# Runs of 64 small products on TensorE, early row mixing on VectorE, and a loop of 28 steps in an RWKV layer with experts

## The chip, the cores and the metric

One Trainium2 chip, one core of it. The metric is the device time of one execution in microseconds (us). The kernel before has a median of 6792.22 us over three runs (6789.73 to 6812.12).

## The reference, what matters of it

The layer has two parts. The first is a time-mixing layer over x of 2 x 4096 rows of 512 channels: rows are mixed with the row before them (`xx = xprev - x`, `xxx = x + xx * time_maa_x`, a small network that gives four deltas, and four mixed inputs `x + xx * (time_maa + delta)`), projected to r, k, v, a gate and several low-rank terms, and run through a recurrence for each of 16 heads of 32 channels:

```
sab = S @ kk
S = S * exp(w) + sab b^T + v k^T
y = S @ r
```

The output is normalised by head, gets a bonus term and the gate, and is projected. The second part is a layer norm with a balanced assignment of 1024 rows to each of 8 experts (512 to 2048 to 512, gelu). The change is in the first part alone.

## The kernel before

The first part goes over 64 tiles. A tile is 64 rows of each of the two sequences, 128 rows together, and lies in memory as 128 channels by 4 groups of 128 columns. The recurrence is solved in chunks of 32 rows: for each of 16 units (group, sequence, chunk) and 4 heads there is a triangular 32x32 system, whose inverse is built by doubling in four levels. A level `lev` is, for each of the 64 systems, a product P (`ub` by `inv`) on TensorE (`P_of`, L842), a copy of it out of PSUM on ScalarE (`part_of`, L605), a product Q (that copy by `invT`) on TensorE (`Q_of`, L858), and on VectorE a masked copy into `invT` (step C.T) and a transposition to `inv` (step C.I) (`invert`, L400). Each product is a 32x32 tile of the array, so that four heads run side by side.

The work is a pipeline over turns. In one turn five stages run, each on another tile: N (row statistics), A (mixing and projections), B (keys, queries and scores for the inverse and the outputs), C (the inverse and the recurrence) and D (norm, gate, output). `step` (L1121) writes one turn for all engines. The order on each engine is written out by hand: in `on_vector` (L340), `on_scalar` (L601), `on_gpsimd` (L762) and `on_tensor` (L821), each of which executes in order, and in the lists `DVE_STEPS`, `ACT_STEPS`, `POOL_STEPS` and `PE_STEPS` that number the steps. A wait on a step is a wait on a semaphore of its engine. PSUM banks are shared in the order of the table `BANK`; `clear` (L333) waits until the last reader of a bank's previous tenant is done.

Five turns are written out, then a loop with a body of four turns runs 14 times, then seven turns are written out (L1138 to L1147). `SETS = 4` sets of semaphores rotate, so the body is a multiple of four.

TensorE's order in a turn, with the names used below: transposition of x (L956, step A.x); a quarter of the values (L829); the first half of P0 (L853, 32 products); a quarter of the values; centre (L969); the second half of P0; mix (L977), which needs VectorE's xxx (L444); the scores for the experts (L983); Q0 (L864) in halves around values; var (L995), delta (L932), gate; P1 in halves around values; bonus (L1016); gate1 and low_wa (both L838), which need the mixed inputs xf0 and xf1 (L398); delta3; Q1 in halves around the score block u0 (L877); u1, u2; P2 in halves around low_k (L838, needs xf2); key (L829); Q2 in halves around u3; key; P3 in halves around decay (L1055); u4, u5; Q3 in halves around low2 (L1071); y0, y1; then the recurrence over two chunks (L891, L905, L915, L924) with y2 to y5, the output projection (L947) and receptance between.

VectorE's order at the start of a turn: query and key spans B.dq, B.dk3, B.dk2 (L349, L354); N's statistics (L436, L438); xx and xxx (L441, L444); B.dk1, B.dk0; keys kb3, kk3 (L360, L363); rated (L457); invert(0); mixed input 0 (L392, L398); D.normed; keys 2; mixed input 1; keys 1 and 0; bonus (L477); C.uk (L413); D.bonus (L483), D.gated (L487); the mask of u0 (L377); invert(1); mixed input 2; mask of u1; mixed input 3, and so on.

Of the kernel before, what the change touches and what calls it, by code (L numbers as in the profile page):

```python
# [8 lines left out]
P = 128  # L9
# [9 lines left out]
SETS = 4  # L19

# [95 lines left out]
def time_mix(nc, core, dram):  # L116
# [3 lines left out]
    with ExitStack() as ctx:  # L120
# [119 lines left out]
        for g in range(G):  # L240
# [16 lines left out]
            "A.carried A.x B.ek3 B.ek012 C.P0 A.mix D.squares B.eq D.lnv N.lnv D.rstd N.rstd B.v C.P1 A.hid_g A.hid_w A.hid_a "  # L257
# [5 lines left out]
            "A.x D.centre C.P0 A.mix A.scored C.Q0 D.var A.delta D.gate B.value C.P1 B.bonus A.gate1 A.low_wa A.delta3 B.u0 C.Q1 "  # L263
            "B.u1 B.u2 A.low_k C.P2 B.u3 C.Q2 A.key A.decay C.P3 B.u4 B.u5 A.low2 C.Q3 B.y0 B.y1 A.sums C.z0 B.y2 "
            "B.y3 C.u0 C.y0 D.out B.y4 B.y5 C.z1 C.u1 A.recept C.y1").split()
# [74 lines left out]
        def on_vector(e, turn, on, out, got):  # L340
# [88 lines left out]
            enter(e, dve, "dve", turn)  # L429
            if Bs:  # L430
                query_span()
                key_span(3)
                key_span(2)
# [5 lines left out]
            if A:  # L439
                e.wait_ge(act.sem, act["A.x"])  # L440
                e.tensor_tensor(by_b(xx), xs[:, :, :, 0:TB], xnow, ALU.subtract).then_inc(dve.sem, dve.step("A.xx"))  # L441
                e.wait_ge(dve.sem, dve["A.xx"])
                for g in range(G):
                    e.scalar_tensor_tensor(  # L444
                        grp(xxx, g).rearrange("p (b t) -> p b t", b=B), grp(xx, g).rearrange("p (b t) -> p b t", b=B),
                        wt["maa_x"][:, g:g + 1], xs[:, g, :, 1:TB + 1], ALU.mult, ALU.add).then_inc(
                        dve.sem, dve.step(f"A.xxx{g}"))
# [20 lines left out]
            if Bs:  # L468
                make_keys(2)
            if A:  # L470
                lerp_of(1)
            if Bs:
                make_keys(1)
                make_keys(0)
                e.wait_ge(act.sem, act["B.v"])
                e.wait_ge(pe.sem, pe["B.bonus"])
                e.tensor_tensor(col(bonuses[(turn - 1) % SETS]), col(BANK["bonus"]), col(v), ALU.mult).then_inc(  # L477
                    dve.sem, dve.step("B.bonus"))
            if Cs:
                turn_scores([(1, "uk")])  # L480
# [7 lines left out]
            if Bs:  # L488
                mask_scores("u", 0)
            if Cs:  # L490
                invert(1)
            if A:
                lerp_of(2)
            if Bs:
                mask_scores("u", 1)
# [105 lines left out]
        def on_scalar(e, turn, on, out, got):  # L601
# [26 lines left out]
            if Bs:  # L628
                e.wait_ge(dve.sem, dve["B.dk3"])
                e.activation(key_units(1, 3), key_units(1, 3), ACT.Exp).then_inc(act.sem, act.step("B.ek3"))  # L630
                e.wait_ge(dve.sem, dve["B.dk0"])
                e.activation(by_key[:, :, 1, 0:key_at(3)], by_key[:, :, 1, 0:key_at(3)], ACT.Exp).then_inc(
                    act.sem, act.step("B.ek012"))
            if Cs:
                part_of(0)
            if A:
                e.wait_ge(pe.sem, pe["A.mix"])
                e.activation(col(mix), BANK["mix"][:, 0:P], ACT.Tanh).then_inc(act.sem, act.step("A.mix"))
            if D:
# [181 lines left out]
        def on_tensor(e, turn, on, out, got):  # L821
# [20 lines left out]
            def P_of(lev, half):  # L842
                if half == 0:
                    clear(e, f"P{lev}")
                    if lev == 0:
                        if "C.rows1" in dve.was:
                            e.wait_ge(dve.old, dve.ago("C.rows1"))
                        e.wait_ge(dve.old, dve.ago("B.inv"))
                    else:
                        e.wait_ge(dve.sem, dve[f"C.I{lev - 1}"])  # L850
# [4 lines left out]
                if half:  # L855
                    mm.then_inc(pe.sem, pe.step(f"C.P{lev}"))

            def Q_of(lev, half):  # L858
                if half == 0:
                    clear(e, f"Q{lev}")  # L860
                    e.wait_ge(act.sem, act[f"C.P{lev}"])
                for n in range(half * U // 2, (half + 1) * U // 2):
# [3 lines left out]
                if half:  # L866
                    mm.then_inc(pe.sem, pe.step(f"C.Q{lev}"))
# [103 lines left out]
            if Cs:  # L971
                P_of(0, 1)
# [13 lines left out]
            if Cs:  # L986
                Q_of(0, 0)
            if Bs:
                value_of(2, 3)
            if Cs:  # L990
                Q_of(0, 1)
# [14 lines left out]
            if Cs:  # L1006
                P_of(1, 0)
            if Bs:
                value_of(3, 4).then_inc(pe.sem, pe.step("B.value"))
            if Cs:  # L1010
                P_of(1, 1)
# [11 lines left out]
            if Cs:  # L1023
                Q_of(1, 0)
            if Bs:
                score("u", 0)
            if Cs:
                Q_of(1, 1)
            if Bs:
                score("u", 1)  # L1030
                score("u", 2)
            if Cs:
                P_of(2, 0)
            if A:
                low("low_k", 2)
            if Cs:
                P_of(2, 1)
            if A:
                clear(e, "key")
                key_of(0, 2)  # L1040
            if Cs:
                Q_of(2, 0)
            if Bs:
                score("u", 3)
            if Cs:
                Q_of(2, 1)
            if A:
                key_of(2, 4).then_inc(pe.sem, pe.step("A.key"))
            if Cs:
                P_of(3, 0)  # L1050
# [7 lines left out]
            if Cs:  # L1058
                P_of(3, 1)
# [3 lines left out]
            if Cs:  # L1063
                Q_of(3, 0)
# [9 lines left out]
            if Cs:  # L1074
                Q_of(3, 1)
# [25 lines left out]
            if Bs:  # L1101
                score("y", 4)
                score("y", 5)
# [606 lines left out]
```

## Time and profile before

| what | value |
|---|---|
| median of three runs | 6792.22 us |
| the profiled execution's own time | 6799.37 us |
| its span, first to last instruction | 6797.6 us |
| granted TensorE clock, mean over the span | 0.949 |
| first part, TensorE transposes x of tile 0 at | 31.7 us |
| the same of the last tile at | about 4661 us |
| busy over the span: PE, PEld, DVE, ACT, POOL | 89%, 64%, 59%, 28%, 21% |

How to read it: PE is TensorE's matmuls, PEld its weight loads, DVE is VectorE, ACT is ScalarE, POOL is GpSimd, SP is SyncE. A turn of the pipeline is counted from one transposition of x (L956) to the next. The matmul of an fp32 product shows as two records and two weight loads, so 32 products are "x64". "idle before" in brackets is the time in which the engine had nothing to run, and after the arrow stands what ended it; "issue" there means that nothing in the profile was waited for, PEq and DVEq are the sequencers, and L329 is the wait at the entry of a turn.

### The profile page before, as it was taken

The numbers are of one execution on the slowest core, as the hardware profiler recorded it, in microseconds if no ns is written. First come the engines' busy times: TensorE is split into PE (matmuls) and PEld (weight loads), VectorE is DVE, ScalarE is ACT, GpSimd is POOL, SyncE is SP. The second block draws the span as 40 slices with busy tenths as digits, with TensorE's granted clock in tenths as the row PEclk, the third lists the DMA queues.
The fourth block names the chain that finished last, engine by engine and source line by source line (L and its number), as shares of the span: only waits on it lengthen the run. The fifth ranks groups of instructions, "written<-read, shape, count | busy, mean of one in ns | idle before, by whom it ended". The sixth has DMA issues, their size and how long they took to land. (4 is left out here: it accounts for less than half of the span.)

```text
span 6797.6 us, 270041 instructions
## 1 busy us (share of the span) xinstructions
PE 6026.9 (89%) x123464; PEld 4343.0 (64%) x123464; DVE 4002.5 (59%) x9325; ACT 1878.1 (28%) x3531; POOL 1458.2 (21%) x1284
## 2 busy tenths in 40 slices
PE   6888888888889888888888888888489999999999
PEld 5777777777777777777777777777334444444444
DVE  5777777777777777777777777777442223222310
ACT  3333333333333333333333333333100000000000
POOL 1222122222212222221222222222021122112220
PEclk8999999999999999999999999999689999999999
DMA  1000000000000000000000000000212211221120
GB/s 54 16 20 16 16 22 16 16 18 20 16 16 22 16 16 18 20 16 17 21 16 16 18 20 16 17 21 11 69 44 70 77 55 62 71 67 65 56 76 13
DMA packets 108728, 212.84 MB, mean 31 GB/s; under 512 B 25424, under 2 KB 26704, under 8 KB 107088
## 3 DMA queue, kind: packets, MB, share of 16 engines
q1 hardware_dynamic: 92240, 144.98, 7.4%
q0 software_dynamic: 15360, 50.48, 2.2%
q8 instruction: 995, 16.30, 1.0%
q14 instruction: 133, 1.09, 0.1%
HBM read 144.67 MB, written 50.72 MB: 29 GB/s over the span
## 5 line engine op out<-in xcount | busy, mean ns | idle before, releaser
L377 DVE COPY_PREDICATED time_raw<-time_known,w_bank 128x96 f32<-128x96 int32 (+6 forms) x3072 | 826.0, 273 | 226.5 <-PE w_bank L877 146.8
L1662 PE MATMUL moe_bank<-moe_w,moe_hidden 128*128 128x512 f32 x2048 | 928.7, 596 | 0.0
L1649 PE MATMUL moe_bank<-moe_hT,moe_w 128*128 128x512 f32 x2048 | 923.2, 594 | 0.8 <-DVE moe_hT L1549 0.8
L1649 PEld LDWEIGHTS moe_bank<-moe_hT,moe_w 128*128 128x128 f32 x2048 | 386.3, 190 | 471.2 <-issue 470.1
L1662 PEld LDWEIGHTS moe_bank<-moe_w,moe_hidden 128*128 128x128 f32 x2048 | 379.4, 190 | 429.5 <-issue 428.1
L1570 ACT ACTIVATE moe_hidden<-moe_bank,moe_b 128x512 f32<-128x512 f32 x256 | 175.9, 687 | 1628.2 <-PE moe_bank L1649 1523.1
L806 POOL TENSOR_TENSOR time_tail<-time_tail,time_lp 128x512 f32<-128x512 f32 x64 | 75.4, 1178 | 2414.1 <-ACT time_lp L733 2350.3
L864 PE MATMUL w_bank<-time_invT,time_part 32*32 32x32 f32 x32768 | 437.1, 204 | 71.5 <-issue 50.2
L402 DVE COPY_PREDICATED time_invT<-time_levels,w_bank 128x512 f32<-128x512 int32 x256 | 187.1, 731 | 499.7 <-PE w_bank L864 499.7
L864 PEld LDWEIGHTS w_bank<-time_invT,time_part 32*32 32x32 f32 x32768 | 373.0, 116 | 152.9 <-issue 98.3
L853 PE MATMUL w_bank<-time_inv,time_ub 32*32 32x32 f32 x32768 | 401.5, 196 | 77.6 <-ACT time_yT L617 30.6
L853 PEld LDWEIGHTS w_bank<-time_inv,time_ub 32*32 32x32 f32 x32768 | 342.3, 107 | 195.2 <-issue 117.1
L774 POOL TENSOR_TENSOR time_queries_u<-time_dq,time_kkn 32x512 f32<-32x512 f32 x256 | 304.4, 1189 | 553.1 <-ACT time_dq L648 538.0
L877 PE MATMUL w_bank<-time_keys,time_queries_u 128*128 128x160 f32 x2048 | 385.1, 329 | 34.8 <-DVE time_mixed L487 14.5
L877 PE MATMUL w_bank<-time_keys,time_queries_y 128*128 128x160 f32 x2048 | 338.7, 313 | 59.0 <-DVE time_mixed L552 53.0
L877 PEld LDWEIGHTS w_bank<-time_keys,time_queries_y 128*128 128x128 f32 x2048 | 290.3, 193 | 121.6 <-DVE time_mixed L552 104.3
L1549 DVE COPY moe_hT<-moe_bank 128x512 f32<-128x512 f32 x64 | 44.2, 691 | 535.6 <-PE moe_bank L1636 535.6
L829 PE MATMUL w_bank<-time_xf,time_value 128*128 128x128 f32 x2048 | 355.8, 328 | 0.1
L774 POOL TENSOR_TENSOR time_queries_y<-time_dq,time_r 32x512 f32<-32x512 f32 x256 | 349.4, 1365 | 26.2 <-POOL time_queries_u L774 10.8
L877 PEld LDWEIGHTS w_bank<-time_keys,time_queries_u 128*128 128x128 f32 x2048 | 306.5, 201 | 63.4 <-DVE time_mixed L487 20.1
L392 DVE SCALAR_TENSOR_TENSOR time_lerp<-w_bank,time_maa,time_xx 128x128 f32<-128x128 f32 x1024 | 284.5, 339 | 64.5 <-PE w_bank L932 64.4
L829 PEld LDWEIGHTS w_bank<-time_xf,time_value 128*128 128x128 f32 x2048 | 307.8, 230 | 9.6 <-PE w_bank L924 0.2
(227 smaller groups left out, 10038.5 us busy)
## 6 DMA issues: line engine op xcount, KB each, us to landing
moe_w<-in_w SPq DMA_DIRECT2D x64, 1024.0 KB, 7.3
mid_xn<-time_xn_rows SPq DMA_DIRECT2D x128, 129.0 KB, 2.5
time_x_rows<-in_x SPq DMA_DIRECT2D x128, 128.0 KB, 2.8
time_base<-in_x SPq DMA_DIRECT2D x128, 128.0 KB, 3.3
mid_acc<-time_mixed SPq DMA_DIRECT2D x128, 128.0 KB, 2.7
mid_scores<-time_rated SPq DMA_DIRECT2D x128, 2.0 KB, 2.2
moe_b<-in_b SPq DMA_DIRECT2D x8, 256.0 KB
time_receptance<-in_w_receptance SPq DMA_DIRECT2D x1, 1024.0 KB, 4.8
```

Source lines behind the costliest of these rows:

```text
L377: e.copy_predicated(by_raw[:, "uy".index(q), n0:n1, :, 0:8 * j + 8], known[:, "uy".index(q), :, :, mine].to_broadcast([P, n1 - n0, 2, 8 * ...
L392: e.scalar_tensor_tensor(grp(lerp, g), grp(BANK[f"delta{f}"], g), wt["maa"][:, f * G + g:f * G + g + 1], grp(xx, g), ALU.add, ALU.mult).th ...
L402: e.copy_predicated(chunks(got["invT"]), level(lev + 1, U), chunks(BANK[f"Q{lev}"])).then_inc(dve.sem, dve.step(f"C.T{lev}"))
L774: e.tensor_tensor(heads_of(q)[head(h), :, h], by_block(dq)[head(h), :, :, at:at + 8], eights(by)[head(h)], ALU.mult).then_inc(pool.sem, po ...
L806: e.tensor_tensor(chunks(tail), chunks(tail), padded(lp)[:, :, 1:33], ALU.add).then_inc(pool.sem, pool.step("A.lt"))
L829: mm = e.matmul(ps[:, o * P:(o + 1) * P], weight[:, g * width + o * P:g * width + (o + 1) * P], rhs_of(g), start=g == 0 and (o == 0 or not ...
L853: mm = e.matmul(BANK[f"P{lev}"][head(h), blk(n)], got["ub"][head(h), blk(n)], got["inv"][head(h), blk(n)], start=True, stop=True, skip_gro ...
L864: mm = e.matmul(BANK[f"Q{lev}"][head(h), blk(n)], part[head(h), blk(n)], got["invT"][head(h), blk(n)], start=True, stop=True, skip_group_c ...
L877: mm = e.matmul(BANK[f"{q}{m}"][:, (n - n0) * 2 * KEYS:(n - n0 + 1) * 2 * KEYS], queries[q][:, n * P:(n + 1) * P], keys[:, n * 2 * KEYS:(n ...
L1570: e.activation(hidden[now % 4][:, :], up[now % 3][:, :], ACT.Gelu_apprx_tanh, bias=b1[:, x * FC + k:x * FC + k + 1]).then_inc(act.sem, act ...
L1649: got = e.matmul(up[now % 3][:, :], w1[:, g * F + k * P:g * F + (k + 1) * P], hT[x % 2][:, g * CAP + half * HALF:g * CAP + (half + 1) * HA ...
L1662: got = e.matmul(down[t][:, :], hidden[now % 4][:, t * P:(t + 1) * P], tile(w2, k), start=k == 0, stop=k == FC - 1)
```

## The change

1. `P_of` and `Q_of` lose their halves: the 64 products of a level stand in one run. What lay between two halves now lies before or after.
2. TensorE's order is rewritten: both first quarters of the values come before P0, centre after it; value(3,4) after P1; u0 and u1 after Q1, then P2, low_k, the first half of key, u2, Q2, the second half of key, u3, P3, decay, u4, u5, Q3, low2. y5 comes before y4.
3. VectorE computes xx and xxx first in a turn, ahead of the spans and the statistics. Mixed input 1 comes ahead of keys 2. invert(1) and mixed input 2 come ahead of C.uk and of the masks of u0 and u1.
4. ScalarE does the copy of P0 and the tanh of mix ahead of the exponential B.ek012, which waits for B.dk0.
5. The loop has a body of 28 turns, executed twice, instead of four turns 14 times.

```diff
+LONG = 28
@@ VectorE
             enter(e, dve, "dve", turn)
+            if A:
+                ...
             if Bs:
                 query_span()
                 key_span(3)
...
+            if A:
+                lerp_of(1)
             if Bs:
                 make_keys(2)
-            if A:
-                lerp_of(1)
-            if Bs:
                 make_keys(1)
                 make_keys(0)
...
-            if Cs:
-                turn_scores([(1, "uk")])
             if D:
                 ...
+            if Cs:
+                invert(1)
+            if A:
+                lerp_of(2)
+            if Cs:
+                turn_scores([(1, "uk")])
             if Bs:
                 mask_scores("u", 0)
-            if Cs:
-                invert(1)
-            if A:
-                lerp_of(2)
-            if Bs:
                 mask_scores("u", 1)
@@ ScalarE
                 e.activation(key_units(1, 3), key_units(1, 3), ACT.Exp).then_inc(act.sem, act.step("B.ek3"))
+            if Cs:
+                part_of(0)
+            if A:
+                ...
             if Bs:
                 e.wait_ge(dve.sem, dve["B.dk0"])
                 ...
-            if Cs:
-                part_of(0)
-            if A:
-                ...
@@ TensorE
-            def P_of(lev, half):
...
-                for n in range(half * U // 2, (half + 1) * U // 2):
+            def P_of(lev):
...
+                for n in range(U):
                     for h in range(HG):
                         mm = e.matmul(BANK[f"P{lev}"][head(h), blk(n)], got["ub"][head(h), blk(n)], got["inv"][head(h), blk(n)],
...
-                value_of(0, 1)
-            if Cs:
-                P_of(0, 0)
-            if Bs:
-                value_of(1, 2)
+                value_of(0, 2)
+            if Cs:
+                P_of(0)
...
             if Bs:
+                score("y", 5)
                 score("y", 4)
-                score("y", 5)
@@ loop
-        with nc.Fori(0, tiles // SETS - 2) as four:
-            for i in range(SETS):
-                step(four * SETS + (i + 1), SETS + 1 + i, "NABCD")
+        turns = (tiles - 8) // LONG
+        with nc.Fori(0, turns) as part_of_tiles:
+            for i in range(LONG):
+                step(part_of_tiles * LONG + (i + 1), SETS + 1 + i, "NABCD")
```

## Rows read from the trace of the kernel before

**Rows 1.** Windows: stretch, us; busy PE, PEld, DVE, ACT, POOL; clock; DMA.
```profile
200.00:4661.00 4461.00, 3904.05 (x110999) 3257.69 (x110996) 3228.78 (x7800) 1581.32 (x3060) 1027.89 (x900) 0.95 0.07 18
```
**Rows 2.** Waits of PE in 200:4661: who for whom, us in total, times, longest.
```profile
PE w_bank L977 <- DVE time_lerp L444: 133.6, 53, 2.8
PE w_bank L838 <- DVE time_xf L398: 79.5, 60, 2.1
PE w_bank L838 <- DVE time_raw L377: 58.6, 60, 1.0
PE w_bank L877 <- DVE time_mixed L552: 51.3, 60, 0.9
PE w_bank L956 <- PEq L329: 46.3, 13, 3.8
PE w_bank L864 <- issue: 43.9, 47, 1.7
PE w_bank L853 <- issue: 19.4, 24, 1.2
```
**Rows 3.** Windows of two turns: the first after a jump back, the other not.
```profile
2064.00:2134.50 70.50, 64.67 (x1850) 53.91 (x1850) 51.70 (x127) 25.72 (x49) 15.98 (x14) 0.95 0.08 19
2208.40:2283.80 75.40, 64.81 (x1850) 54.15 (x1850) 53.32 (x131) 26.49 (x51) 16.95 (x15) 0.95 0.07 17
```
**Rows 4.** Timeline, PE, a turn without jump: start, length, what, [idle before].
```profile
1689.53 0.66 PE L956 MATMUL w_bank<-time_ident,time_xn_rows 128*128 128x128 f32 x4
...
1697.62 1.41 PE L977 MATMUL w_bank<-time_lerp,time_maa_w 128*128 128x128 f32 x8 [2.79 <-DVE time_lerp L444]
...
1701.37 2.08 PE L829 MATMUL w_bank<-time_xf,time_value 128*128 128x128 f32 x8
```
**Rows 5.** Timeline, PE, start of a turn after a jump back.
```profile
2064.30 1.08 PE L956 MATMUL w_bank<-time_ident,time_xn_rows 128*128 128x128 f32 x4 [3.36 <-PEq L329]
...
2074.59 1.16 PE L829 MATMUL w_bank<-time_xf,time_value 128*128 128x128 f32 x8
```
**Rows 6.** Timeline, PE, halves of a level and what lies between them.
```profile
1728.52 0.75 PE L864 MATMUL w_bank<-time_invT,time_part 32*32 32x32 f32 x64
1729.21 2.05 PE L829 MATMUL w_bank<-time_xf,time_key_w 128*128 128x128 f32 x16
1731.19 0.75 PE L853 MATMUL w_bank<-time_inv,time_ub 32*32 32x32 f32 x64
...
1733.64 1.35 PE L877 MATMUL w_bank<-time_keys,time_queries_u 128*128 128x160 f32 x8
1735.48 0.82 PE L864 MATMUL w_bank<-time_invT,time_part 32*32 32x32 f32 x64 [0.48 <-ACT time_part L607]
...
1737.37 0.55 PE L864 MATMUL w_bank<-time_invT,time_part 32*32 32x32 f32 x41
1739.33 0.39 PE L864 MATMUL w_bank<-time_invT,time_part 32*32 32x32 f32 x23 [1.41 <-issue]
```
**Rows 7.** Timeline, DVE, the start of the turn of rows 4.
```profile
1692.32 0.72 DVE L427 TENSOR_TENSOR time_state<-time_grown,time_faded 128x256 f32<-128x256 f32 x1
...
1696.33 1.14 DVE L444 SCALAR_TENSOR_TENSOR time_lerp<-time_xx,time_maa_x,time_x 128x128 f32<-128x128 f32 x4
...
1698.64 0.69 DVE L363 TENSOR_TENSOR time_keys<-time_keys,time_k 128x512 f32<-128x512 f32 x1
...
1710.39 1.44 DVE L363 TENSOR_TENSOR time_keys<-time_keys,time_k 128x384 f32<-128x384 f32 x1
...
1714.83 0.68 DVE L477 TENSOR_TENSOR time_bonus<-w_bank,time_v 128x512 f32<-128x512 f32 x1
```
**Rows 8.** Timeline, ACT, the copy of P0 in that turn.
```profile
1698.79 0.57 ACT L607 COPY time_part<-w_bank 128x512 f32<-128x512 f32 x1
```
**Rows 9.** The page: busy time and records; a DMA queue's packets, MB, share.
```profile
PE 6026.9 (89%) x123464; PEld 4343.0 (64%) x123464; DVE 4002.5 (59%) x9325; ACT 1878.1 (28%) x3531; POOL 1458.2 (21%) x1284
...
q8 instruction: 995, 16.30, 1.0%
```

More of the change, by code:

```diff
@@ L256, in time_mix @@
         ACT_STEPS = (
-            "A.carried A.x B.ek3 B.ek012 C.P0 A.mix D.squares B.eq D.lnv N.lnv D.rstd N.rstd B.v C.P1 A.hid_g A.hid_w A.hid_a "
+            "A.carried A.x B.ek3 C.P0 A.mix B.ek012 D.squares B.eq D.lnv N.lnv D.rstd N.rstd B.v C.P1 A.hid_g A.hid_w A.hid_a "
             "D.affine0 D.affine1 D.affine2 D.affine3 A.hid_kkk A.hid_mk C.P2 A.exp_z A.tail A.k C.P3 A.tna A.tnma "
@@ L262, in time_mix @@
         PE_STEPS = (
-            "A.x D.centre C.P0 A.mix A.scored C.Q0 D.var A.delta D.gate B.value C.P1 B.bonus A.gate1 A.low_wa A.delta3 B.u0 C.Q1 "
-            "B.u1 B.u2 A.low_k C.P2 B.u3 C.Q2 A.key A.decay C.P3 B.u4 B.u5 A.low2 C.Q3 B.y0 B.y1 A.sums C.z0 B.y2 "
-            "B.y3 C.u0 C.y0 D.out B.y4 B.y5 C.z1 C.u1 A.recept C.y1").split()
+            "A.x C.P0 D.centre A.mix A.scored C.Q0 D.var A.delta D.gate C.P1 B.value B.bonus A.gate1 A.low_wa A.delta3 C.Q1 B.u0 "
+            "B.u1 C.P2 A.low_k B.u2 C.Q2 A.key B.u3 C.P3 A.decay B.u4 B.u5 C.Q3 A.low2 B.y0 B.y1 A.sums C.z0 B.y2 "
+            "B.y3 C.u0 C.y0 D.out B.y5 B.y4 C.z1 C.u1 A.recept C.y1").split()
         BANK = Banks(psum, [
@@ L429, in on_vector @@
             enter(e, dve, "dve", turn)
+            if A:
+                e.wait_ge(act.sem, act["A.x"])
+                e.tensor_tensor(by_b(xx), xs[:, :, :, 0:TB], xnow, ALU.subtract).then_inc(dve.sem, dve.step("A.xx"))
+                e.wait_ge(dve.sem, dve["A.xx"])
+                for g in range(G):
+                    e.scalar_tensor_tensor(
+                        grp(xxx, g).rearrange("p (b t) -> p b t", b=B), grp(xx, g).rearrange("p (b t) -> p b t", b=B),
+                        wt["maa_x"][:, g:g + 1], xs[:, g, :, 1:TB + 1], ALU.mult, ALU.add).then_inc(
+                        dve.sem, dve.step(f"A.xxx{g}"))
             if Bs:
@@ L438, in on_vector @@
                 e.bn_aggr(mv[:, :], stats[:, :]).then_inc(dve.sem, dve.step("N.mv"))
-            if A:
[L440 to L447, printed above, removed]
             if Bs:
@@ L467, in on_vector @@
                 e.tensor_tensor(col(mixed), col(BANK["centre"]), col(rstd), ALU.mult).then_inc(dve.sem, dve.step("D.normed"))
-            if Bs:
-                make_keys(2)
             if A:
@@ L472, in on_vector @@
             if Bs:
+                make_keys(2)
                 make_keys(1)
@@ L487, in on_vector @@
                 e.tensor_tensor(col(mixed), col(mixed), col(BANK["gate"]), ALU.mult).then_inc(dve.sem, dve.step("D.gated"))
-            if Bs:
-                mask_scores("u", 0)
             if Cs:
@@ L493, in on_vector @@
                 lerp_of(2)
+            if Cs:
+                turn_scores([(1, "uk")])
             if Bs:
+                mask_scores("u", 0)
                 mask_scores("u", 1)
@@ L630, in on_scalar @@
                 e.activation(key_units(1, 3), key_units(1, 3), ACT.Exp).then_inc(act.sem, act.step("B.ek3"))
-                e.wait_ge(dve.sem, dve["B.dk0"])
-                e.activation(by_key[:, :, 1, 0:key_at(3)], by_key[:, :, 1, 0:key_at(3)], ACT.Exp).then_inc(
-                    act.sem, act.step("B.ek012"))
             if Cs:
@@ L638, in on_scalar @@
                 e.activation(col(mix), BANK["mix"][:, 0:P], ACT.Tanh).then_inc(act.sem, act.step("A.mix"))
+            if Bs:
+                e.wait_ge(dve.sem, dve["B.dk0"])
+                e.activation(by_key[:, :, 1, 0:key_at(3)], by_key[:, :, 1, 0:key_at(3)], ACT.Exp).then_inc(
+                    act.sem, act.step("B.ek012"))
             if D:
@@ L840, in low @@
                 mm.then_inc(pe.sem, pe.step("A." + name))
-            def P_of(lev, half):
[L843 to L850, printed above, removed]
-                for n in range(half * U // 2, (half + 1) * U // 2):
+            def P_of(lev):
+                clear(e, f"P{lev}")
+                if lev == 0:
+                    if "C.rows1" in dve.was:
+                        e.wait_ge(dve.old, dve.ago("C.rows1"))
+                    e.wait_ge(dve.old, dve.ago("B.inv"))
+                else:
+                    e.wait_ge(dve.sem, dve[f"C.I{lev - 1}"])
+                for n in range(U):
                     for h in range(HG):
@@ L854, in P_of, with Q_of @@
                                       start=True, stop=True, skip_group_check=True)
[L855 to L862, printed above, removed]
+                mm.then_inc(pe.sem, pe.step(f"C.P{lev}"))
+            def Q_of(lev):
+                clear(e, f"Q{lev}")
+                e.wait_ge(act.sem, act[f"C.P{lev}"])
+                for n in range(U):
                     for h in range(HG):
@@ L865, in Q_of @@
                                       start=True, stop=True, skip_group_check=True)
-                if half:
-                    mm.then_inc(pe.sem, pe.step(f"C.Q{lev}"))
+                mm.then_inc(pe.sem, pe.step(f"C.Q{lev}"))
             def score(q, *which):
@@ L970, in on_tensor @@
                     pe.sem, pe.step("D.centre"))
-            if Cs:
-                P_of(0, 1)
             if A:
@@ L986, in on_tensor @@
             if Cs:
-                Q_of(0, 0)
+                Q_of(0)
             if Bs:
                 value_of(2, 3)
-            if Cs:
-                Q_of(0, 1)
             if D:
@@ L1006, in on_tensor @@
             if Cs:
-                P_of(1, 0)
+                P_of(1)
             if Bs:
                 value_of(3, 4).then_inc(pe.sem, pe.step("B.value"))
-            if Cs:
-                P_of(1, 1)
             if Bs:
@@ L1023, in on_tensor @@
             if Cs:
-                Q_of(1, 0)
+                Q_of(1)
             if Bs:
                 score("u", 0)
+                score("u", 1)
             if Cs:
[L1028 to L1033, printed above, removed]
+                P_of(2)
             if A:
                 low("low_k", 2)
-            if Cs:
-                P_of(2, 1)
             if A:
@@ L1040, in on_tensor @@
                 key_of(0, 2)
+            if Bs:
+                score("u", 2)
             if Cs:
-                Q_of(2, 0)
+                Q_of(2)
+            if A:
+                key_of(2, 4).then_inc(pe.sem, pe.step("A.key"))
             if Bs:
@@ L1045, in on_tensor @@
             if Cs:
-                Q_of(2, 1)
-            if A:
-                key_of(2, 4).then_inc(pe.sem, pe.step("A.key"))
-            if Cs:
-                P_of(3, 0)
+                P_of(3)
             if A:
@@ L1057, in on_tensor @@
                 mm.then_inc(pe.sem, pe.step("A.decay"))
-            if Cs:
-                P_of(3, 1)
             if Bs:
@@ L1063, in on_tensor @@
             if Cs:
-                Q_of(3, 0)
+                Q_of(3)
             if A:
@@ L1073, in on_tensor @@
                 mm.then_inc(pe.sem, pe.step("A.low2"))
-            if Cs:
-                Q_of(3, 1)
             if Bs:
```

8 rows, old and new, of the table DVE_STEPS are left out of this document.

## The prediction

> **What bounds the kernel now.** I read first how the time divides: one window over the 60 full turns of the first part. It holds 4461 us, 74.4 us a turn, and TensorE is busy for 3904 of them, VectorE for 3229 (53.8 a turn), ScalarE and GpSimd for far less [rows 1]. The rest of the span, the experts and the ends, is untouched but for the few turns at both ends, which I leave out. So the question is a turn of TensorE, times 60. It is not all work: each turn has some 9 us without a matmul, and the clock is 0.95 on average, which is a tenth of the time at 1.2 GHz instead of 2.4, some 3.7 us of work lost in a turn of 74.4.
>
> Second, the waits of PE, divided by 60 [rows 2]. The largest is that of mix (L977) for xxx, 133.6 us, 2.2 a turn, and nearly 2.8 in each turn without a jump. Then low_wa for xf1, 79.5 (1.3); low_k for xf2, listed under the mask that ran just after it, 58.6 (1.0); y4 for the addition into acc, 51.3 (0.85); the jump back, 46.3 (13 times 3.6). The rows named "issue" wait for no other engine: 43.9 and 19.4, 1.06 a turn.
>
> Third, two turns side by side [rows 3]: the one after a jump takes 70.5 us, the other 75.4, with the same busy PE to 0.2 us. The turn after the jump is short because VectorE has caught up: mix has no wait of 2.79. The jump's cost is thus largely given back in this kernel, and taking it away alone would bring little. It is worth its price only because xxx is also made earlier.
>
> Fourth, the clock. In the turn without a jump TensorE idles before mix, and then the 8 records of the values at L829 take 2.08 us [rows 4]; after a jump the same 8 take 1.16 [rows 5]. The slow stretch at the start follows that idle time.
>
> **The change part by part**, in us of a turn, against 74.4.
>
> *xx and xxx first.* VectorE ends the last turn's state at 1693.04, 3.5 after TensorE's L956 at 1689.53; from xx to mix it is two steps, 0.69 (taken from a step of equal size, L363) and 1.14, with the hand-over some 2.0 [rows 4, 7]. Mix can start at 5.5 instead of 8.1. Ahead of it TensorE has the transposition (0.5), 16 records of values (1.98), P0 (1.2, below) and centre (about 1.0): 4.7. A wait of about 1.0 stays, with ends 0.5 and 1.5. Against 2.2 and a wait of the first half of P0 of about 0.5 for the last copy of the turn before, now covered by the second quarter of the values: **-1.7**.
>
> *The jump.* 12 of 13 go: 46.3 x 12/13 / 60 = **-0.7**. The rest of each body was streamed before as it is now: 16.3 MB over the queue of instructions, about 66 bytes for each of TensorE's 247 thousand matmul and load records [rows 9], more than a body of four could keep.
>
> *The clock.* If the idle stretch before mix shrinks to 1.0, the slow stretch behind it should mostly go; other gaps of 1.0 to 1.4 us stay, and new ones come. Ends: nothing, and all 3.7. I take **-2.0**.
>
> *Runs of 64.* The second half of a run costs what its records cost inside one: x64 takes 0.75 and x41 takes 0.55, 8.7 ns each, so 0.56 for 64, against a start-to-start of 0.69 for a half [rows 6]. The neighbours join too: 16 records take 2.05 and 8 take 1.16, so one visit less saves 0.2 (2 x 1.16 less 2.05, less the overlap of 0.07 of lengths) [rows 5, 6]. Together 0.13 + 0.2 = 0.33, eight times: **-2.6**. Ends: 0.1 and 0.4 each, -0.8 and -3.2.
>
> *Mixed input 1 ahead of keys 2.* These keys are 0.9 and 1.44 long [rows 7], so xf1 comes 2.3 earlier and low_wa's 1.3 go: **-1.3**. Low_k: xf2 is ready some 1.8 after C.I1 ends, and P2 covers 1.2 of it instead of 0.7: **-0.4**. y5 ahead of y4 puts 0.65 under the wait of 0.85 for acc, but then the copy of y out of PSUM is barely late: **-0.4**.
>
> New waits. *Q0* needs the copy of P0, on ScalarE behind the exponential of dk3, which VectorE now makes after xxx: 5.35 for xxx, two spans 1.25, exponential 0.65, copy 0.57 [rows 8], hand-overs: 8.0. TensorE is at 7.4. **+0.6**, ends 0 and 1.4. *u0* needs the bonus and all keys. From the end of delta TensorE has gate, P1, values, bonus, gate1, low_wa, delta3 and Q1: six visits of about 1.05 and two runs, 8.7. VectorE has xf0, normed, xf1, six key steps and the bonus: 8.7 to 10. The spread is what POOL does to it: the key step of 384 columns took 1.44 beside the queries of GpSimd, the one of 512 took 0.69 without [rows 7]. **+1.0**, ends 0.2 and 1.6. *Q3*: ScalarE comes to the copy of P3 after three operations on decay and key. Now Q3 waits 0.48 with half of P3 and u4, u5 ahead of it [rows 6]; the half is gone from there: **+0.8**, ends 0 and 1.3. The masks of u0 come later than C.T1 and xf2 but before u2 needs their bank: nothing. SyncE waits for rated and acc as before, and neither moves by more than 1 us: nothing.
>
> *Instructions.* The stalls named issue fall in the dense places: 23 records of Q3 came 1.41 late, in the middle of a run [rows 6]. A product is four PE records here; at 66 bytes a record a packet of 16 KB is about 250 of them, which is one run of 64 products. 995 packets take 1.0% of 16 engines, 1.1 us each [rows 9]. A turn needs 3700 records, 15 packets, one per 4.6 us at a turn of 69; a run now eats one in 1.2 us, a half ate half of one in 0.7. Stalls now cost 1.06; I take them to double and a little: **+1.2**. The ends are -1.06 (all gone) and 8 x 1.41 less 1.06, +10.2, if each run stops once; I stay near today's rows as the mean demand grows by only 8%.
>
> The Trainium skill speaks to this place: Runtime: NRT & Kernel Launch, section Instruction fetch mechanics, says that instructions come in blocks of 16 KiB, that crossing into the next is mostly hidden, and that a taken branch out of the window costs a fetch. The 3.36 of idle time at the jump agrees. The 1.41 inside straight code does not, and by the page alone the +1.2 would be 0 or less; that is the second rival below.
>
> Sum: -1.7 - 0.7 - 2.0 - 2.6 - 1.3 - 0.4 - 0.4 = -9.1; +0.6 + 1.0 + 0.8 + 1.2 = +3.6; net -5.5, a turn of 68.9. Sixty turns: -330. The profiled execution took 6799.4, so 6469; it lies 7 above the median, so **6462**.
>
> **The rivals.**
> First, **instructions bound the runs** (slower). Each run of 64 products stops once for its packet, as Q3 did, 1.41 each: 11.3 a turn instead of 2.3. The net is then +3.5 to the turn, +210: about 7000. It decides from 6.7 a turn of added stall, 0.8 for each run. For it: the stalls stand in dense places already. Against: only 71 issue waits of 0.9 on average over 60 turns in these two rows, with 16 half runs a turn. 4%.
> Second, **instructions are hidden**: the stalls go away with the idle places before the runs as slack: 2.3 less a turn, 66.6: 6325. For it: the other waits let the sequencer run ahead; against: the 1.41. 12%.
> Third, **VectorE becomes what is late**: 53.8 busy in 69 is 78%, and its order is a chain with TensorE's. If the bonus comes 1.6 late and its delay carries into u1, P2, low_k with another 1.5, the turn is 71.0: 6590. For it: the slowed key steps; against: its idle time at Q0 and Q2 is several us. 16%.
> Fourth, **the clock does not recover**: gaps of 1.0 before mix, 0.6 before Q0, then four around u0 to low_k, keep as much of the turn at 1.2 GHz: +2.0, 6582. 13%.
>
> **How the numbers follow.** The forecast has 55%, the rivals 4, 12, 16 and 13. The unknown costs around the forecast (clock 1.7 either way, runs 1.0, u0 and Q3 1.0, instructions 1.0) come to about 2.3 a turn together, 140 us. 6340 to 6620 holds the third and fourth rival and most of the forecast's spread. About 0.3% is what a measurement of this kernel can tell from no change; only the first rival is slower by that, and no change would need the terms to cancel: 95% faster, 1% same, 4% slower.
>
> **What would show it.** Right: mix's wait near 1.0 and none of 2.8; low_wa without a wait; turns all alike with no jump but one; clock of a turn at 0.97 or more; rows of 128 records for P and Q in about 1.3; issue waits of about 2 a turn. Wrong: Q and P rows broken in two by issue waits of over 1 in most turns (first rival); a wait of u0 for the bonus beyond 1.6 and of low_k beyond 1 (third); a clock of 0.95 (fourth).

## The result: 6739.6 us against 6792.2, and 6462 was forecast

The changed kernel takes 6739.57 us (median of five runs, 6734.03 to 6745.69), a ratio of 0.9918 to the kernel before, 95% interval 0.9901 to 0.9934. It is faster, as forecast, but by 53 us, 0.8%, and not by 330, and it lies outside the stated range of 6340 to 6620. The profiled execution took 6739.65 us, its span is 6737.7 us, the mean clock 0.937 against 0.949.

First the window over the same 60 turns as [rows 1], in the kernel after.

```profile
197.50:4596.80 4399.30, 3840.92 (x111001) 3249.24 (x111001) 3298.81 (x7801) 1571.59 (x3060) 1024.52 (x900) 0.93 0.07 18
```

A turn is 73.3 us against 74.4; forecast were 68.9. The busy time of PE fell by 63 us, 1.05 a turn; the time in which it idles is 557 us before and 558 after, 9.3 a turn. The clock is 0.93, not higher than 0.95. So nothing of the idle time was won. Of the work more was won than the busy time shows: busy time times clock, as an estimate, is 61.8 us a turn before and 59.5 after, but the lower clock took about half of that back. The waits of PE show where the idle time went; columns as in [rows 2], stretch 200:4600, nearly the window above.

```profile
PE w_bank L852 <- issue: 132.6, 82, 2.8
PE w_bank L861 <- issue: 113.3, 77, 2.8
PE w_bank L861 <- DVE time_raw L378: 59.9, 53, 1.4
PE w_bank L873 <- DVE time_bonus L477: 44.3, 34, 2.1
PE w_bank L969 <- DVE time_lerp L436: 40.7, 38, 1.3
PE w_bank L1051 <- issue: 28.7, 16, 2.7
PE w_bank L861 <- ACT time_part L606: 21.0, 45, 0.7
PE w_bank L873 <- DVE time_mixed L551: 19.3, 60, 0.7
...
PE w_bank L829 <- issue: 17.6, 19, 2.5
PE w_bank L838 <- DVE time_xf L399: 14.4, 39, 0.5
...
PE w_bank L952 <- PEq L330: 3.5, 1, 3.5
```

Against [rows 2]: mix (now L969) waits 40.7 us instead of 133.6, low_wa and low_k (L838) 14.4 instead of 138.1, y4 (after L551) 19.3 instead of 51.3, the jump 3.5 instead of 46.3. All the rows that name another engine or the jump come to 237 us, 4.0 a turn; they were 447, 7.5 a turn. And all the rows "issue" come to 313 us, 5.2 a turn, where before they were 98, 1.6 a turn. (Q3's wait for ScalarE's copy of P3 stands in the row of time_raw L378: a mask happened to end last before it.) What the other engines gave back went into stalls in which TensorE waits for none of them.

The timeline of PE shows where they stand; in brackets the idle time before.

```profile
1253.78 1.50 PE L829 MATMUL w_bank<-time_xf,time_key_w 128*128 128x128 f32 x12
1255.12 0.98 PE L873 MATMUL w_bank<-time_keys,time_queries_u 128*128 128x160 f32 x6
1256.04 1.29 PE L852 MATMUL w_bank<-time_inv,time_ub 32*32 32x32 f32 x128
1257.25 0.38 PE L1037 MATMUL w_bank<-time_hid_w,time_decay_w 96*128 96x128 f32 x1
1259.15 1.47 PE L1037 MATMUL w_bank<-time_hid_w,time_decay_w 96*128 96x128 f32 x7 [1.53 <-issue]
1260.42 2.34 PE L873 MATMUL w_bank<-time_keys,time_queries_u 128*128 128x160 f32 x8
1263.08 1.13 PE L861 MATMUL w_bank<-time_invT,time_part 32*32 32x32 f32 x111 [0.32 <-DVE time_raw L378]
1266.46 0.44 PE L861 MATMUL w_bank<-time_invT,time_part 32*32 32x32 f32 x17 [2.26 <-issue]
1266.83 2.09 PE L1051 MATMUL w_bank<-time_hid,time_low_w 32*128 32x128 f32 x32
```

P3 (L852) runs through in 1.29 us, the price that the prediction put on a run: 128 records in one piece, against two pieces of 0.75 with their visits. One record of decay later TensorE stands for 1.53 us. It does 7 records of decay, 8 of u4 and u5 and 111 of Q3 and stands again, 2.26 us, in the middle of a run. From stall to stall that is 126 matmul records; a window over it counts 127 weight loads as well:

```profile
1259.15:1266.46 7.31, 4.73 (x126) 4.26 (x127) 2.66 (x9) 2.25 (x4) 0.00 (x0) 0.77 0.01 2
1314.30:1322.72 8.42, 4.80 (x126) 4.02 (x127) 8.11 (x19) 0.00 (x0) 0.73 (x2) 0.80 0.01 2
```

The second row is the same between two other stalls, in the middle of Q1 and in the middle of P2, with the same counts. 253 records and a few semaphore instructions are one packet of the instruction queue: the page gives it 977 packets with 16.01 MB, so 16.4 KB each, and 64 to 66 bytes a record. The stalls stand where one packet ends. Counted with the semaphore instructions, all 159 issue stalls of more than 0.8 us in the 60 turns lie whole multiples of 256 instructions apart, with one shift, at the jump. A packet ends in a place, not after a time: in the second row TensorE ran out of instructions 7.0 us after the packet's first record, with two waits for VectorE in between, and the next packet was late by 1.42 us all the same.

The DMA view shows when the late packets move. The first line is 1259.15:1264.10, the next two 1264.10:1264.20:

```profile
DMA packets 0, 0.00 MB, mean 0 GB/s; under 512 B 0, under 2 KB 0, under 8 KB 0
DMA packets 1, 0.02 MB, mean 164 GB/s; under 512 B 0, under 2 KB 0, under 8 KB 0
q8 instruction: 1, 0.02, 59.1%
```

So the packet starts at 1264.1, when TensorE has all but finished the one before it; TensorE stands from 1264.20 and goes on at 1266.46. In the second case nothing moves in 1314.30:1320.40 and one packet starts in 1320.40:1320.50; TensorE stands from 1321.3 and goes on at 1322.72. Other transfers can't have held these two up, as there were none. In all 159 stalls TensorE goes on 2.2 to 2.9 us after such a packet starts, and 1.2 to 1.7 us after it ends.

Behind these two stalls the clock falls. A window before them, one behind each, and what lies between (last columns: clock, DMA share, GB/s):

```profile
1251.00:1257.00 6.00, 6.00 (x273) 5.62 (x273) 5.21 (x15) 0.00 (x0) 0.00 (x0) 1.00 0.02 5
1259.70:1263.10 3.40, 3.08 (x17) 2.71 (x16) 1.24 (x6) 2.25 (x4) 0.00 (x0) 0.51 0.00 0
1263.10:1266.40 3.30, 1.10 (x111) 1.01 (x112) 1.43 (x4) 0.00 (x0) 0.00 (x0) 1.00 0.02 5
1266.50:1269.90 3.40, 3.40 (x53) 3.11 (x53) 2.04 (x3) 0.91 (x2) 0.00 (x0) 0.51 0.02 5
1270.00:1276.00 6.00, 6.00 (x149) 4.83 (x148) 3.18 (x11) 2.50 (x7) 0.00 (x0) 1.00 0.16 46
1322.72:1326.12 3.40, 3.40 (x51) 3.35 (x51) 2.92 (x10) 1.21 (x3) 0.00 (x0) 1.00 0.02 5
```

In the stretches behind the two the clock is 0.51, the lower of its two levels, 1.2 and 2.4 GHz. Not every stall does this: the last row is the stretch behind the stall of 1.42 us, at 1.00. The 8 records of u4 and u5 took 2.34 us in such a stretch; before they took 1.35 [rows 6].

### The profile page after: what moved, and what is told of

Read it like the earlier page. It is cut to its first block and busy times, and to the rows that moved or that the text cites. A ratio compares the mean times of both kernels' runs of the same rounds, so it can differ in the third digit from the quotient of the medians.

```text
span 6737.7 us, 269852 instructions
## 1 busy us (share of the span) xinstructions
PE 5964.4 (89%) x123464; PEld 4335.2 (64%) x123464; DVE 4075.9 (60%) x9325; ACT 1868.0 (28%) x3531; POOL 1454.5 (22%) x1284
## 3 DMA queue, kind: packets, MB, share of 16 engines
q8 instruction: 977, 16.01, 1.0%
## 5 line engine op out<-in xcount | busy, mean ns | idle before, releaser
L378 DVE COPY_PREDICATED time_raw<-time_known,w_bank 128x96 f32<-128x96 int32 (+6 forms) x3072 | 828.4, 275 | 429.6 <-PE w_bank L873 343.6
L861 PE MATMUL w_bank<-time_invT,time_part 32*32 32x32 f32 x32768 | 362.8, 197 | 211.7 <-issue 122.1
L852 PE MATMUL w_bank<-time_inv,time_ub 32*32 32x32 f32 x32768 | 364.8, 197 | 155.1 <-issue 134.8
L861 PEld LDWEIGHTS w_bank<-time_invT,time_part 32*32 32x32 f32 x32768 | 326.2, 107 | 259.6 <-issue 163.2
L852 PEld LDWEIGHTS w_bank<-time_inv,time_ub 32*32 32x32 f32 x32768 | 326.8, 108 | 209.0 <-issue 193.5
L774 POOL TENSOR_TENSOR time_queries_u<-time_dq,time_kkn 32x512 f32<-32x512 f32 x256 | 312.0, 1219 | 484.5 <-ACT time_dq L648 469.5
L873 PE MATMUL w_bank<-time_keys,time_queries_y 128*128 128x160 f32 x2048 | 382.2, 335 | 28.3 <-DVE time_mixed L551 19.9
L873 PEld LDWEIGHTS w_bank<-time_keys,time_queries_u 128*128 128x128 f32 x2048 | 330.2, 214 | 96.5 <-DVE time_bonus L477 56.9
L873 PEld LDWEIGHTS w_bank<-time_keys,time_queries_y 128*128 128x128 f32 x2048 | 329.3, 211 | 91.6 <-issue 39.0
L829 PE MATMUL w_bank<-time_xf,time_value 128*128 128x128 f32 x2048 | 303.3, 300 | 12.2 <-issue 12.1
L829 PE MATMUL w_bank<-time_xf,time_key_w 128*128 128x128 f32 x2048 | 288.3, 299 | 6.8 <-issue 6.8
```

The source lines that it names most:

```text
L378: e.copy_predicated(by_raw[:, "uy".index(q), n0:n1, :, 0:8 * j + 8], known[:, "uy".index(q), :, :, mine].to_broadcast([P, n1 - n0, 2, 8 * ...
L774: e.tensor_tensor(heads_of(q)[head(h), :, h], by_block(dq)[head(h), :, :, at:at + 8], eights(by)[head(h)], ALU.mult).then_inc(pool.sem, po ...
L829: mm = e.matmul(ps[:, o * P:(o + 1) * P], weight[:, g * width + o * P:g * width + (o + 1) * P], rhs_of(g), start=g == 0 and (o == 0 or not ...
L873: mm = e.matmul(BANK[f"{q}{m}"][:, (n - n0) * 2 * KEYS:(n - n0 + 1) * 2 * KEYS], queries[q][:, n * P:(n + 1) * P], keys[:, n * 2 * KEYS:(n ...
```

## Experiments

Eleven kernels ran. Each has a ratio to the kernel before on the same chip. The theory: runs of 64 products take their instructions faster than packets come, and the stalls pull the clock down. The rivals: the new order of steps costs it, VectorE or ScalarE is late anyway, or the jumps were not worth removing.

**1. TensorE's order of before, the rest of the change.**

```diff
-                value_of(0, 2)
-            if Cs:
-                P_of(0)
+                value_of(0, 1)
+            if Cs:
+                P_of(0, 0)
+            if Bs:
+                value_of(1, 2)
...
```

> The changed kernel, but TensorE's order and the halves of P and Q as before (so VectorE's and ScalarE's new order and the loop of 28 stay). Theory: runs of 64 products (256 records) eat a packet of instructions faster than the next one comes, 5.3 us of issue waits a turn, and the idle places lower the clock. With halves the issue waits go back to about 1.6 a turn, the clock to 0.95 or more, mix and low_wa keep their short waits: a turn of 69 to 71, 6530 to 6620 us. Rival (runs of 64 are worth their 2.6 us a turn and the moved steps cost it): 2.6 us a turn slower than the change, about 6890.

Measured: 6908.58 us, ratio 1.0171 [1.0144, 1.0199]. The theory's number failed and the rival's was met, but for a reason that neither had. The waits of PE (200:4600):

```profile
PE w_bank L877 <- DVE time_raw L378: 205.1, 58, 4.2
PE w_bank L877 <- DVE time_bonus L477: 140.4, 57, 3.2
PE w_bank L864 <- issue: 65.3, 54, 1.7
```

The issue waits did fall, to some 1.8 us a turn. But in TensorE's old order u0 comes half a run earlier and u2 before P2, while VectorE now masks u0 after mixed input 2. So u0 waits 2.5 us a turn for the bonus, and u2 3.5 for the mask. The two orders belong together; this kernel undid too much at once. It shows that VectorE's later masks don't go with TensorE's old order; it says nothing of runs against halves.

**2 and 3. The loop.** A body of 4 in the changed kernel, and a body of 28 in the kernel before.

```diff
-LONG = 28
+LONG = 4
```

> The changed kernel with a loop body of 4 turns, executed 14 times. Theory: each jump back costs 3.5 us, 12 more of them 42; with xx first the turn after a jump wins little back (1 us each): 6765 to 6785. Rival (as in the kernel before, the turn after a jump gives all of it back): 6740.

> The kernel before with the loop of 28 turns and nothing else. Theory: the 12 jumps (3.5 us each, 42) go, but the 12 turns after them lose their head start (70.5 against 74.5): 6785 to 6805, no change. Rival: the jumps' time is gained, 6750.

Measured: 6755.19 us (6733.47 to 6768.89), 0.9936 [0.9914, 0.9959], against 0.9918 [0.9901, 0.9934] of the change; and 6787.65, 0.9992 [0.9982, 1.0003]. In the kernel before the loop is worth nothing, as its head start after a jump is paid back. In the changed kernel it is worth 16 us between medians, with intervals that overlap: between what the two expectations said, and not settled beyond "less than the 42 of the jumps". Its jumps take 44.5 us (PEq, 13 times), and part of that comes back: over its 60 turns mix waits 27.3 us in all instead of 40.7, and the issue rows come to 304 instead of 313.

**4 and 5. Few records.** Each run of 64 products becomes ten, and then five, products of 128x128x128. The inverse is left out in these two; all other steps stay.

```diff
-                for n in range(U):
-                    for h in range(HG):
-                        mm = e.matmul(BANK[f"P{lev}"][head(h), blk(n)], got["ub"][head(h), blk(n)], got["inv"][head(h), blk(n)],
+                for n in range(10):
+                    mm = e.matmul(BANK[f"P{lev}"][:, n % G * P:(n % G + 1) * P], grp(got["ub"], n % G), grp(got["inv"], n % G),
```

> The changed kernel with each run of 64 products of 32x32 (256 records of TensorE) replaced by 10 products of 128x128x128 (40 records), about as long (1.1 us); it leaves the inverse out, its levels are computed from other products. A turn has 1700 fewer records, all else is the same. Theory (instructions bound the runs, and their stalls pull the clock down): issue waits below 1 us a turn, clock 0.97 or more, a turn of 67 to 69.5, 6380 to 6520 us. Rival (the other engines are what is late, and TensorE would wait for them anyway): issue waits turn into waits for VectorE and ScalarE, a turn of 72 to 73, 6690 to 6740.

> As the run with ten products, but five of 128x128x128 (10 matmul records of 0.11 us, 1.1 us) in the place of each run of 64; ten were 2.2 us and so 1 us a run too long, 8 us a turn. The inverse is left out. Theory: no issue waits, clock 0.98 or more, and the 8 us fall away but for what VectorE and ScalarE are then late: a turn of 64 to 68, 6170 to 6420 us. Rival (the full clock of the run with ten products came from its longer work, not from the missing stalls): clock 0.95 or less and a turn of 68 to 70, 6420 to 6550.

Measured: 6545.97 us, 0.9639 [0.9613, 0.9665], with ten, just outside the 6380 to 6520 that were expected; 6317.12 us, 0.9298 [0.9280, 0.9317], with five. Ten had been sized wrongly: they last 2.2 us, a run 1.2, so that kernel carries 8 us more work a turn and is still 194 us faster than the change. Its clock over the turns is 1.00. With five, which are nearly as long as a run, it is 422 us. Nearly: from start to start five take 1.14 us and a run 1.22, and neighbours are a little shorter too. Busy time times clock, as an estimate, is 57.9 a turn against 59.5, so some 100 of the 422 us are less work and not fewer stalls. Its largest waits of PE (200:4100):

```profile
PE w_bank L871 <- DVE time_bonus L477: 146.2, 59, 2.6
PE w_bank L859 <- DVE time_raw L378: 80.4, 59, 1.4
PE w_bank L967 <- DVE time_lerp L436: 77.3, 57, 1.4
...
PE w_bank L899 <- issue: 2.0, 5, 0.8
```

The issue waits are gone: 2.4 us over all turns. VectorE's part returned, 2.5 us a turn at u0, so the whole of 5.2 is not free to have. A window of its 60 turns:

```profile
191.13:4190.22 3999.09, 3581.84 (x54361) 3084.48 (x54361) 3381.26 (x7802) 1571.96 (x3060) 1042.02 (x900) 0.97 0.07 18
```

66.7 us a turn, in the range that was expected; the clock is 0.97, just short of the 0.98 expected. With ten it was 1.00, and there u0 waits 32 us in all instead of 146: with longer work VectorE is late less, so part of that full clock did come from the longer work.

**6. Halves in the new order.** Only the runs are undone, each half beside the step that stood next to the run.

```diff
             if Cs:
-                Q_of(2)
+                Q_of(2, 0)
             if A:
                 key_of(2, 4).then_inc(pe.sem, pe.step("A.key"))
+            if Cs:
+                Q_of(2, 1)
```

> The changed kernel with P and Q in halves again, but around the step that stands next to each run in the new order, so that no other step moves: the runs of 64 alone are undone. The halves cost 0.33 us each time, 2.6 a turn. Theory (runs starve for instructions): issue waits fall from 5.3 us a turn to 2 to 2.5 and the clock rises from 0.93 to 0.95 or more; a turn of 71.5 to 73, 6630 to 6720 us, faster than the change. Rival (the stalls depend on how many records there are and not on how they are bunched): 2 to 3 us a turn slower than the change, 6860 to 6900.

Measured: 6552.14 us, 0.9636 [0.9615, 0.9657], faster than even the theory expected. This is the verdict on the runs, with all their records on both sides: they cost the change 187 us, 3.1 a turn, where the prediction gave them -2.6 + 1.2. It is also the best full kernel of this study, 3.6% faster than before. Its window of 60 turns and its issue waits (200:4400):

```profile
190.85:4424.20 4233.35, 3836.53 (x111000) 3216.95 (x111000) 3332.90 (x7801) 1578.93 (x3060) 1038.26 (x900) 0.96 0.08 19
```

```profile
PE w_bank L877 <- DVE time_bonus L477: 92.9, 57, 2.2
PE w_bank L864 <- issue: 70.5, 69, 1.8
PE w_bank L853 <- issue: 41.2, 55, 1.5
```

PE is busy for 3837 us, as in the changed kernel (3841), though it makes 16 visits a turn instead of 8: the higher clock pays for the visits. By busy time times clock, an estimate, the visits are some 2 us of work a turn. The issue waits are 2.1 us a turn, 3.2 less, the largest single one 1.8 instead of 2.8.

**7. Runs of 64 in the kernel before**, at the place of the second half.

```diff
                 if half == 0:
+                    return
+                if half == 1:
                     clear(e, f"P{lev}")
...
-                for n in range(half * U // 2, (half + 1) * U // 2):
+                for n in range(U):
```

> The kernel before with each level in one run of 64 products, put where the second half stood; nothing else moves. Theory: 2.6 us a turn of work goes and 2.5 to 3.5 of issue waits come, the clock falls by 0.01 to 0.02: 6790 to 6880. Rival (runs are a gain and something else of the change loses it): 6640 to 6700.

Measured: 6877.99 us, 1.0131 [1.0107, 1.0155]. As expected, the runs cost there too, 83 us between medians. The issue waits are 2.9 us a turn instead of 1.6, the largest 2.2; the clock of its profile is 0.927, that of the kernel before 0.949.

**8. xx and xxx first in the kernel before**, with ScalarE's order of the change: xx and xxx (first left-out part) ahead of the spans and statistics of VectorE, the copy of P0 and A.mix ahead of B.ek012 on ScalarE.

```diff
             if A:
...
+            if Bs:
+                query_span()
+                key_span(3)
+                key_span(2)
...
```

> The kernel before with VectorE's xx and xxx ahead of the spans and statistics, and ScalarE's copy of P0 and tanh ahead of the second exponential; TensorE's order, the halves and the loop of 4 as before. Theory: the wait of mix (2.2 us a turn) falls to 0.5 to 1 and with it the slow stretch of clock behind it: 1.5 to 3.5 us a turn, 6590 to 6710. Rival (what is won at mix comes back at the next wait, since the spans and keys are 2 us later): 6770 to 6800.

Measured: 6653.36 us, 0.9790 [0.9763, 0.9816]. This part alone is worth 141 us, 2.4 a turn, as expected. The wait of mix falls to 8.8 us in all (200:4400), and the clock of the turns from 0.95 to 0.97. Low_wa still waits 81.5 us, as its input is made where it was before.

**9. Places of halves without their records.** The counterpart of five products, in three and two at the places of experiment 6; the inverse is left out here too.

```diff
-                for n in range(5):
+                for n in range(3 * half, 3 + 2 * half):
```

> The version with halves in the new order, with three and two products of 128x128x128 in the place of the halves of each run; the inverse is left out, as in the run with five products, to which it is the counterpart: the same places of the pieces as with 32 products, but a ninth of their records. Halves against one run were worth 187 us with the full records (6552 against 6740). Theory (that is instructions alone): with few records nothing is left of it, within 40 us of the 6317 of the run with five products, either side. Rival (the halves win by their place, because a run behind a neighbour covers or ends a wait): 6317 less 100 to 190, 6130 to 6220.

Measured: 6372.14 us, 0.9363 [0.9345, 0.9380]. It is 55 us slower than five in one piece between medians, 44 by the ratios, as the two ran on different chips. So whether it is beyond the 40 that the theory allowed isn't settled, but it lies on the side away from the rival. With few records the pieces' places don't win; one piece is a gain of 0.7 to 0.9 us a turn. With 256 records a run is a loss of 3.1. This gain isn't the price of a visit in the real kernel: the stand-ins are 128x128 products like most of their neighbours, and the halves are 32x32 products.

**10 and 11. Two tries at a better version.** The first, on experiment 6, puts delta ahead of var. The second is built on the first: it moves a quarter of key from Q2 into P3 and decay behind P3.

```diff
+            if A:
...
+                delta_of(0, 1, 2).then_inc(pe.sem, pe.step("A.delta"))
             if D:
                 clear(e, "var")
```

> The version with halves in the new order, and on TensorE delta ahead of var (1.05 us earlier), for the wait of u0 for VectorE's bonus, 1.6 us a turn there, with a slow stretch of clock of 3.4 us or more behind it in each turn. VectorE's chain from delta to the bonus starts 0.6 to 1 us earlier. Theory (that wait is set by VectorE's chain, and the slow stretch by the wait): the wait falls to 0.6 to 1, the slow stretch goes in part: 0.8 to 2 us a turn, 6430 to 6510 us. Rival (normed comes later by as much and the bonus with it, or the time comes back as an issue wait): 6540 to 6560.

```diff
-                key_of(2, 4).then_inc(pe.sem, pe.step("A.key"))
+                key_of(2, 3)
...
                 P_of(3, 0)
+            if A:
+                key_of(3, 4).then_inc(pe.sem, pe.step("A.key"))
```

> The same, with a quarter of key moved from between the halves of Q2 to between the halves of P3 (decay behind both), so that large products thin out the dense place around Q3, where half of the issue waits stand. Theory (packets are late where records are bunched): issue waits from 2.1 to 1.2 to 1.7 us a turn, 20 to 60 us faster than the version with delta first. Rival (the stalls only move to Q2 or elsewhere): no difference beyond 15 us.

Measured: 6579.14 us, 0.9681 [0.9653, 0.9709], and 6645.69 us, 0.9783 [0.9756, 0.9810]: neither is better, and both miss their expectations on the slow side. The second is 67 us slower than the first, where 20 to 60 us faster were expected. With delta first u0's wait did fall by half, to 44.8 us (200:4400), and the turns' clock rose to 0.98. But this row is new:

```profile
PE w_bank L829 <- ACT time_sq L651: 46.7, 60, 0.8
```

It is the gate's product, which takes the bank of var and now stands right behind it: it waits for ScalarE to read var. Low_wa and low_k wait 39.3 us instead of 24.3, and P 13.1 instead of 2.8 for C.I. With the quarter of key moved Q3 waits 78.4 us for ScalarE's copy of P3 (the row names time_raw, but the copy ends 0.15 us before Q3 starts), as A.k and the copy come later, and the issue rows don't change (128 us against 127, 197:4200). The clock is 0.98 in both, so a higher clock doesn't make up for new waits.

## Why the prediction was wrong

*Instructions: +1.2 a turn, measured +3.6.* This is the step that failed first. The prediction saw that a run is one packet and that stalls stood in dense places, and wrote the mechanism down as its first rival, with 1.41 per run. It then sized it by the mean demand ("grows by only 8%"). The mean says nothing here: 14.5 packets in 73 us is one per 5 us, and in the two windows above TensorE ran out 5.0 and 7.0 us after a packet's first record. What counts is how much work is left when the next packet starts to move, as TensorE goes on 2.2 to 2.9 us after that, and a run lasts 1.2 us for all its 256 records. The first rival, given 4%, had this mechanism and the sign of it; its size, a stop of 1.41 at each run, was too large, as the stalls come where a packet ends and not at each run. The prediction also counted 1.06 a turn of such waits in the kernel before where all rows give 1.6: it had left out the smaller rows. The Trainium skill, Runtime: NRT & Kernel Launch, section Instruction fetch mechanics, says that crossing a block is mostly hidden. The issue waits of 5.2 us a turn decide against that here. What the Trainium skill says there of block size, 16 KiB, and of a taken branch agrees with 16.4 KB a packet and the 3.5 us of the one jump left.

*Clock: -2.0 a turn, measured a loss.* This is the second step that failed, and it hangs on the first. PE's busy time fell by 1.05 a turn, where -2.0 and -2.6 were forecast, and the clock fell from 0.95 to 0.93. The slow stretch behind mix went: in the turn at 1219 mix and the scores behind it run at full clock after a wait of 1.2. But the stalls for instructions open new ones, as the two above: by a count over the trace some 100 of the 135 slow stretches of the 60 turns follow such a stall. The prediction had said that new gaps would come, put no price on them and took nothing as the worse end. Experiment 8, which has the early xx without the runs, shows the term right in sign: 0.97. Experiment 6 with halves has 0.96; 44 of its 65 slow stretches follow u0's wait.

*Runs: -2.6.* The price of a run was right, 1.22 from start to start against 1.24. Busy time times clock gives some 2 us a turn less work than before, and as much less than experiment 6: near the term and inside its ends. The term is about right as work and wrong as time.

*xx first, the jump, mixed input 1, low_k, y5.* Right as waits. Mix's wait is 0.7 a turn (1.0 forecast), the jump 3.5 in all, low_wa and low_k together 0.2 instead of 2.3, where 1.7 had been forecast as gain, y4 0.3. Together the waits for other engines and the jump fell by 3.5 a turn; the forecast had them fall by 2.1. The jump's gain of 0.7 isn't there in either kernel as time (experiments 2 and 3), which the prediction said of the kernel before and didn't follow through for this one.

*Q0, u0, Q3.* +0.6, +1.0 and +0.8; measured 0.35 (L861 for ScalarE), 0.75 and 1.0, the last the whole wait of Q3, which was 0.24 a turn before. Right within their ends. VectorE's keys beside GpSimd's queries are late for u0, as said: in the turn at 1310 two of 384 columns took 1.54 and 1.44 us and one of 256 took 1.42, beside those queries, where one of 512 without them took 0.69.

Summed: work and clock missed by 3.5 a turn, instructions by 2.4, the other waits were 1.4 better: 4.5, and 73.3 less 68.9 is 4.4. Take the runs away and the forecast comes nearly true for what is left: without its -2.6 and +1.2 it gives 70.3, and experiment 6 measured 70.6. That closeness is in part luck: there too the other waits fell by about 1 more than forecast, and the clock gave less than its 2.0.

## What to carry to other kernels

Count records, not only time: where small products are packed side by side, TensorE can use up a packet of 256 instructions in 1.2 us, and then "issue" rows stand in straight code. Put large products between the pieces, even at a visit's price of about 0.3 us; compare the record counts between stalls with a packet before joining runs, and look in the DMA view for when the instruction packets move. And where two engines' orders are written to match, undo or test them together: TensorE's old order with all of VectorE's new one lost 169 us against the change, though the early xx alone went well with it (experiment 8).

## What the runs showed of the hardware that was not expected

A stall for instructions came 7.0 us after the first record of a packet, in which TensorE had twice waited for VectorE: these waits did not bring the next packet nearer. It started to move 5.0 and 6.1 us after the first record of the one before it in the two cases shown, and TensorE had then started 253 and 140 matmul and load records of that one. So the lateness is a late start and not a slow transfer; from which place in a block the next one is asked for stays open, and no kernel was built for that. Over the 60 turns of the changed kernel TensorE went on 2.2 to 2.9 us after a late packet's start in all 159 stalls of more than 0.8 us, and the same bounds hold for the 62 in the kernel before.

Idle stretches of 1.5 and 2.3 us were each followed by a stretch at 1.2 GHz, one of 1.42 us (to 1322.72) and one of 1.78 us (to 1339.77) were not. So stalls can cost more than their length: experiment 6 has 3.2 us a turn less of them and some 2 us more work, by the estimate above, and is still 2.8 us a turn faster in its window.
